# GpSimd makes the middle products of a bidirectional recurrence, and the decay's factor moves to ScalarE's exponential

## The reference

```python
tf = sigmoid(sum(time_emb, axis=-1))[:, None, None]
decay = exp(-exp(w))[None, :] * (0.5 + 0.5 * tf[:, :, 0])
ek = exp(minimum(k, 30.0));  ekv = ek * v
def step(carry, x):
    a, b = carry
    ekv_t, ek_t = x
    a = a * decay + ekv_t
    b = b * decay + ek_t
    return ((a, b), (a, b))
nf, df = scan(step, ..., (ekv_t, ek_t))                  # over the 256 time steps
nb, db = scan(step, ..., (ekv_t, ek_t), reverse=True)
euk = exp(minimum(u + k, 30.0))
num = nf + nb - ekv + euk * v
den = df + db - ek + euk
base = sigmoid(r) * (num / maximum(den, 1e-08))
out = base * (0.8 + 0.2 * tf)
```

## Time and profile before

| | |
|---|---|
| median of 3 runs | 372.89 us (369.75 to 375.7) |
| the profiled execution's own time | 368.91 us |
| its span on the core | 367.1 us |
| mean granted TensorE clock | 0.823 of full speed |

### The profile page before, as it was taken

How to read it: one execution, slowest core, us unless ns; L and a number is a source line. 1 busy time by engine, 2 the same in 40 slices (tenths; PEclk the granted TensorE clock), 3 DMA queues, 4 the chain that set the end, 5 groups by cost and what they waited for, 6 DMA issues and landing times.

```text
span 367.1 us, 6013 instructions
## 1 busy us (share of the span) xinstructions
PE 264.5 (72%) x2294; PEld 166.2 (45%) x2294; DVE 258.2 (70%) x494; ACT 207.4 (57%) x349; POOL 42.5 (12%) x70
## 2 busy tenths in 40 slices
PE   0053867899896888477885969769498499987645
PEld 0033434556554455244463546545266255565413
DVE  2989888779988999887699296774453535436671
ACT  3847598679859885245278257821675224452422
POOL 2102101021011113000310140103000000000000
PEclk9996586889999999887998598958789555698876
DMA  4905546345876530330036303603000000000000
GB/s 142 414 30 108 101 79 116 59 79 94 192 140 129 111 67 2 57 57 2 1 59 114 59 1 57 116 0 59 1 2 14 14 2 1 2 29 0 17 14 29
DMA packets 8524, 23.58 MB, mean 64 GB/s; under 512 B 1584, under 2 KB 2992, under 8 KB 8112
## 3 DMA queue, kind: packets, MB, share of 16 engines
q0 software_dynamic: 4320, 15.73, 22.7%
q1 hardware_dynamic: 4176, 7.48, 6.0%
HBM read 6.43 MB, written 1.05 MB: 20 GB/s over the span
## 4 chain that ended last, share of the span: by engine, by line
PE 44%; DVE 34%; ACT 11%; issue 9%; DMA 2%; POOL 1%; DVEq 0%; ACTq 0%; POOLq 0%
PE PS L1347 8%; DVE fwd L712 5%; PE PM L1264 5%; DVE bwd L720 4%; PE PO L1362 4%; PE PO L1461 3%; PE PS L1438 2%; PE PM L1090 2%; DVE kp L952 2%; PE PS L1326 2%; PE PO L1145 2%; PE PO L1378 2%; DVE fwd L1003 2%; PE PO L1160 2%; PE PO L1447 2%
## 5 line engine op out<-in xcount | busy, mean ns | idle before, releaser
L952 DVE TENSOR_REDUCE kp<-PS 128x2 f32<-128x256 f32 x64 | 32.3, 549 | 28.5 <-PE PS L1326 28.4
L639 ACT ACTIVATE E<-PS 128x384 f32<-128x384 f32 x64 | 27.9, 490 | 41.0 <-PE PS L1347 41.0
L523 ACT ACTIVATE E<-PS,negc,escale 128x1024 f32<-128x1024 f32 x32 | 38.3, 1201 | 4.7 <-PE PS L1130 4.5
L1090 PE MATMUL PM<-w,sg 128*128 128x256 f32 x32 | 11.3, 516 | 20.9 <-DVE sg L735 20.9
L1347 PE MATMUL PS<-w,TP 32*128 32x256 f32 (+1 forms) x128 | 20.8, 442 | 6.9 <-ACT E L639 6.9
L1145 PE MATMUL PO<-E,kp 128*32 128x256 f32 x256 | 20.3, 441 | 7.6 <-DVE ytok L810 4.1
L329 POOL DMA_DIRECT2D fwd<-bwd x15 | 13.4, 891 | 90.3 <-DVE bwd L720 53.4
L1130 PE MATMUL PS<-TP 32*128 32x256 f16 x256 | 20.3, 284 | 3.6 <-DVE TP L762 3.6
L1347 PEld LDWEIGHTS PS<-w,TP 32*128 32x128 f32 x128 | 15.7, 244 | 14.1 <-issue 9.2
L1264 PE MATMUL PM<-G,sg 128*128 128x512 f32 x32 | 20.1, 786 | 2.0 <-DVE sg L735 2.0
L323 POOL DMA_DIRECT2D fwd<-mid x15 | 13.4, 896 | 69.0 <-DVE fwd L712 69.0
(11 more groups left out here) (188 smaller groups left out, 591.9 us busy)
## 6 DMA issues: line engine op xcount, KB each, us to landing
fwd<-mid POOLq DMA_DIRECT2D x15, 512.0 KB, 4.6
fwd<-bwd POOLq DMA_DIRECT2D x15, 512.0 KB, 4.7
kT<-in_kT SPq DMA_DIRECT2D x4, 256.0 KB, 6.4
xT<-in_xT SPq DMA_DIRECT2D x4, 256.0 KB, 5.5
G<-in_w SPq DMA_DIRECT2D x1, 1024.0 KB, 8.6
vt<-in_w SPq DMA_DIRECT2D x1, 1024.0 KB, 10.4
G<-in_attn SPq DMA_DIRECT2D x1, 1024.0 KB, 6.6
out<-ek SPq DMA_DIRECT2D x8, 128.0 KB, 1.7
```

What stands on the lines that cost most here:

```text
L523: nc.scalar.activation(E[:, p % 6], PS[:, 2 * (p % 2):2 * (p % 2) + 2, :], ACT.Exp, bias=negc[:], scale=escale[:]).then_inc(S["e0_done"], 1)
L639: nc.scalar.activation(E[:, p % 4, i, 0:384], PS[:, i, 0:384], ACT.Exp, scale=QSCALE).then_inc(S["e1_done"], 1)
L952: nc.vector.tensor_reduce(kp[:, b % 2, u * H + 2 * j:u * H + 2 * j + 2, D], PS[:, at0:at0 + 2, lo:hi], AX, ALU.max, negate=True).then_inc( ...
L1090: ins = nc.tensor.matmul(PM[:, 0, u * C:(u + 1) * C], sg[:, seg(b, k * T + u * P, P)], w0[:, 0, k, :], start=(k == 0), stop=(k == HALF - 1))
```

## The change

The product `kT * mid` goes from DVE's `inputs(n)` to POOL's `add_mid(n)` for n = 2 to 15; for n = 0 and 1 it stays on DVE. The factor `fb` is taken out of all products, of `ekv` too, so that they are plain two-input multiplications. It comes back in the reciprocal: ACT's exponential gets the bias ln(fb), and the guard of the gate becomes fb times 1e8, read from a tile by partition. POOL makes `fbmax` and ACT makes `lnfb` once at the start.

```diff
             def add_mid(n):
-                r, o = n % RING, n % 2
+                r, o, b = n % RING, n % 2, n % B
+                if n >= 2:
+                    pool.wait_ge(S["m_done"], n + 1)
+                    nc.gpsimd.tensor_tensor(mid[:, o, 1], kT[:, seg(b)], mid[:, o, 0],
+                                            ALU.mult).then_inc(S["mv_done"], 1)
                 pool.wait_ge(S["mv_done"], n + 1)
                 pool.wait_ge(S["scan_done"], 4 * n + 2)
                 nc.gpsimd.dma_start(fwd[:, r], mid[:, o], accum_op=ALU.add).then_inc(S[f"mid_added{o}"], 16)
...
             nc.gpsimd.tensor_scalar(fb[:], cth[:], 0.05, 0.45, ALU.mult, ALU.add).then_inc(S["decay_ready"], 1)
+            pool.wait_ge(S["decay_ready"], 1)
+            nc.gpsimd.tensor_scalar(fbmax[:], fb[:], 1e8, None, ALU.mult).then_inc(S["fbmax_done"], 1)
             link(nc.gpsimd.tensor_scalar(dtf[:], cth[:], 0.25, 0.75, ALU.mult, ALU.add))
...
-                nc.scalar.activation(fwd[:, r, 0], fwd[:, r, 0], ACT.Exp, scale=-1.0).then_inc(S["rec_done"], 1)
+                nc.scalar.activation(fwd[:, r, 0], fwd[:, r, 0], ACT.Exp, bias=lnfb[:, b:b + 1],
+                                     scale=-1.0).then_inc(S["rec_done"], 1)
...
                     act.wait_ge(S["ln_bias"], 1)
+                    nc.scalar.activation(lnfb[:], fb[:], ACT.Ln).then_inc(S["lnfb_done"], 1)
+                    act.wait_ge(S["lnfb_done"], 1)
                     wkv(0)
...
-                nc.vector.scalar_tensor_tensor(G[l][:, seg(b)], fwd[:, r, 0], 1e8, fwd[:, r, 1], ALU.min,
+                    dve.wait_ge(S["fbmax_done"], 1)
+                nc.vector.scalar_tensor_tensor(G[l][:, seg(b)], fwd[:, r, 0], fbmax[:, b:b + 1], fwd[:, r, 1], ALU.min,
                                                ALU.mult).then_inc(S["gate_ready"], 1)
...
                     dve.wait_ge(S["ek_raw"], b + 1)
-                    dve.wait_ge(S["decay_ready"], 1)
                     link(nc.vector.tensor_scalar(ek[:, seg(b)], ek[:, seg(b)], EXP30, None, ALU.min))
-                    nc.vector.scalar_tensor_tensor(ekv[:, seg(b)], kT[:, seg(b)], fb[:, b:b + 1], ek[:, seg(b)],
-                                                   ALU.mult, ALU.mult).then_inc(S["ekv_done"], 1)
+                    nc.vector.tensor_tensor(ekv[:, seg(b)], kT[:, seg(b)], ek[:, seg(b)],
+                                            ALU.mult).then_inc(S["ekv_done"], 1)
                 dve.wait_ge(S["prep_done"], 3 * n + 2)
                 nc.vector.tensor_scalar(mid[:, n % 2, 0], mid[:, n % 2, 0], EXP30, None,
                                         ALU.min).then_inc(S["m_done"], 1)
-                dve.wait_ge(S["m_done"], n + 1)
-                nc.vector.scalar_tensor_tensor(mid[:, n % 2, 1], kT[:, seg(b)], fb[:, b:b + 1], mid[:, n % 2, 0],
-                                               ALU.mult, ALU.mult).then_inc(S["mv_done"], 1)
+                if n < 2:
+                    dve.wait_ge(S["m_done"], n + 1)
+                    nc.vector.tensor_tensor(mid[:, n % 2, 1], kT[:, seg(b)], mid[:, n % 2, 0],
+                                            ALU.mult).then_inc(S["mv_done"], 1)
```

More of the change, by code:

```diff
@@ L48 @@
     "cond_sum", "cond_tanh", "decay_exp", "ek_raw", "ekv_done", "decay_ready", "decay_edge", "prep_done",
-    "pool_chain", "dve_chain", "pads_set", "kp_clear",
+    "pool_chain", "dve_chain", "fbmax_done", "lnfb_done", "pads_set", "kp_clear",
     "m_done", "mv_done", "scan_done", "den_early", "num_early", "mid_added0", "mid_added1", "back_added0",
@@ L100, in build @@
         dtf = sb("dtf", [P, B])
+        fbmax = sb("fbmax", [P, B])
+        lnfb = sb("lnfb", [P, B])
         ew = sb("ew", [P, LAYERS, HALF])
```

## The result

| | before | after |
|---|---|---|
| time, median of 20 runs each (us) | 368.96 (366.06 to 375.83) | 372.65 (370.18 to 376.24) |
| ratio to before, 95% interval | | 1.0114 (1.0086 to 1.0142) |
| span of the profiled execution (us) | 367.1 | 370.9 |
| mean granted clock of TensorE | 0.823 | 0.813 |
| DVE busy (us) | 258.2 | 259.8 |

Some executions of any kernel fall in a slower state at a lower granted clock (5 of the 20 before, 1 of the 20 after); ratios leave them out, and so the plain medians differ by less, 3.7 us. The change costs 1.1%, 4.2 us. That is under the 2% up to which I had called it no change, but the interval starts at 0.9%, well clear of none. The predicted 372.6 us agrees with the 372.65 only because it stood on a median of three runs, 372.89, that was high: 20 runs of before have 368.96. What has to be compared is the difference, -0.3 us forecast and +4.2 measured.

What follows compares the result with a forecast made beforehand. The prediction took a chain of 44% PE and 34% DVE as the bound. Its terms, -4.7 + 0.35 - 0.07 + 0.3 + 3.8 = -0.3 us, on a median of 372.89 gave 372.6 us, range 367 to 378.

Steps and rivals of the forecast that it cites:

- What POOL's product costs DVE: POOL products of 1.1 us hold DVE's two-input SBUF work; +3.8 us in all, 6.2 at the upper bound.
- Rival (a): DVE held by POOL's products cancels the gain from moving them: 372.6 us, no change; chance 0.50.
- Where the products meet DVE: Costly meetings at n = 2, 6, 7, 9, 10, 11, mostly with scans and gates; n = 12 at 0.
- The price of one: One meeting of a POOL product with DVE's two-input work costs about 0.9 us, bounds 0 and 1.3.
- The relief: Products leaving DVE's part of the chain save 0.78 us each, six of them: -4.7 us.
- the six: Products of n = 2, 6, 7, 10, 11 and 12, the only ones counted on the chain, 0.78 us each.
- the other eight: Products of n = 3, 4, 5, 8, 9, 13, 14 and 15, whose leaving DVE was counted at nothing.
- Gate and fold: Gate limit read from a tile, +0.35 us; plain two-input products, -0.07; the exponential's bias costs nothing.
- The start: `fbmax` between `fb` and `dtf` on POOL delays the first scan 0.27 us; +0.3 with the first gate's 0.07.
- POOL's queue: The product delays add_mid(8) by 1.1 us and add_back(8) by at most that; 1.6 us of slack covers it.
- Rival (c): Slower: the product delays the DMA issued just ahead, add_back lands 1.1 to 1.45 us later; 376.5 us, chance 0.25.
- DVE busy: DVE's busy time in the profile after would fall to about 250 to 255 us, as blocked instructions count as busy.

Runs made afterwards that it cites:

- none_all: Kernel with all products on DVE, but those of n = 2 to 15 left out on every engine; ratio to the kernel before 0.993.
- fold_dve: Changed kernel with all 16 products back on DVE, the rest of the change kept; ratio to the kernel before 1.002, 369.50 us.
- fold_twin: fold_dve with POOL making each product of n = 2 to 15 once more into an unread tile; ratio to the kernel before 1.0449, 383.72 us.
- fold_fill: fold_dve with POOL filling an unread tile for n = 2 to 15, reading nothing from SBUF; ratio to the kernel before 1.0049.
- fold_copy: fold_dve with POOL multiplying one SBUF input by 1.0 into an unread tile for n = 2 to 15; ratio to the kernel before 1.0129.
- fold_start: fold_dve with the old start: `fbmax` made behind the decays, DVE's first clamp waiting for `fb`; ratio to the kernel before 1.001.
- timed_late: Changed kernel, old start, 1 MB load held back, 11 products on POOL timed to miss DVE's two-input SBUF reads, rest on DVE; ratio to before 1.0031, 367.18 us.
- after_spacer: Changed kernel with a one-element fill, waited for, ahead of each product on POOL; ratio to the kernel before 1.0036, 369.65 us.

## Why the prediction was wrong

The forecast of no change failed at the step **"What POOL's product costs DVE"**, the term of +3.8 us. That term took its meetings for the places where the leaving product lay in the chain, and its price from an add with no DMA issue ahead of it. Against none_all it measures 6.8 us, give or take 1.7, so even the lower end is above 3.8. The sum of the terms as measured: relief -3.3, fold with start and gate +0.7, blocks +6.8, together +4.2. (They add up by construction: none_all and fold_dve stand between before and after.)

- **The mechanism was right.** fold_twin, fold_fill and fold_copy show that POOL's reads hold DVE's two-input work, and instructions on the accumulators go free, as the earlier trace rows had it. Rival (a) named the mechanism that decides; its balance was wrong.
- **Where the products meet DVE.** I priced six meetings that cost something, for the values of n whose product lay in the chain and for n = 9. There were 11. For n = 4, 8, 13 and 15 I had written nothing, since the product's *leaving* gains nothing there. A block costs where it falls, and it falls on other instructions (scan, gate) than the one that left. n = 12 was to take the place of a collision that was there, at 0; a block of 0.77 came for the 0.35 that line 702 had lost to the adds. The five meetings that I had at nothing make 5.6 of the 11.2 us.
- **The price of one.** 0.9 us with a bound of 1.3, from 0.48 for an add of 0.72 in the earlier trace rows, was near the mean (11.2 over 11 is 1.02) and wrong at the top: 1.71, 1.35 and 1.75 right behind the issue of add_back. There the add of the earlier trace rows was no guide, for no DMA was issued ahead of it. At the six priced places 3.8 were predicted and 5.6 measured.
- **From durations to time** there is no fixed rate. In fold_twin 12.9 us of blocks cost 15.8 us, in the changed kernel 11.2 cost 6.8. Up to the clearing of `kp` the changed kernel is 8.8 us behind none_all, with 6.5 us of blocks by then. TensorE is granted less there as well (0.74 against 0.81 from 45 to 70 us, 0.94 against 1.00 from 100 to 120). What of the two is cause and what follows stays open.
- **The relief.** -4.7 predicted, -3.3 measured, give or take 2: not contradicted. That the six make up all of it isn't shown either: they gave 1.8 and the other eight 1.0, with the same error.
- **Gate and fold.** +0.35 and -0.07 with the start's 0.3 make 0.6; measured 0.7. The gate takes 0.74 to 0.75 instead of 0.68, as the row of another instruction with such an operand had it. That the bias costs nothing was wrong in the instruction: ACT's exponential takes 0.72 in all 16 places with a bias by partition and took 0.63 without, but it isn't seen in the time of fold_start, 1.001.
- **The start.** +0.27 predicted, 0.97 measured, 0.19 of it from the loads. "That DVE no longer waits for `fb` gains nothing" was too mild: the wait kept two engines apart, and without it `fb`, `fbmax` and `dtf` were stretched. I had applied the rule of the blocks to DVE alone, though the earlier trace rows shows POOL's adds stretched as well.
- **POOL's queue.** Add_mid(8) went out 1.9 us behind its place of none_all, counted from add_back(7) (2.46 against 0.54 us between the starts), for the 1.1 predicted. Add_back(8) went out 1.20 us after gate(7), before 1.29: the slack covered it, as said. Rival (c) forecast slower, by a later landing of add_back; that wasn't seen. The kernel is slower by another way, the blocks.
- **DVE busy.** 250 to 255 predicted, 259.8 measured: the same mis-sizing.

No version that makes all the products was faster than the kernel before. The best of the changed ones, timed_late and after_spacer, lie 0.3 to 0.4% above it with intervals that touch no difference.

## What to carry to other kernels

Before an elementwise instruction goes from VectorE to GpSimd, list for each of its copies what VectorE runs in the 1.3 us behind its new start, all along the program and not only where the old one was on the critical path; each two-input SBUF instruction there can cost the whole of the moved one (here up to 1.75 us for 1.26 behind a DMA issue), and here the blocks cost twice what the move freed. Leave the product out altogether first: if that gives 0.9%, another placement can't be expected to give more. A wait that looks useless may be what keeps the two engines out of each other's way.

## What was not expected of the hardware

- A GpSimd product queued right behind its DMA issue can hold a VectorE instruction that is listed ahead of it, by 0.23 us at 93.07 in the changed kernel and by 0.42 at 93.52 in fold_twin; these lost 1.71 and 1.88 us to a product of 1.26. With a one-element fill and a wait between them no scan lost more than 1.08.
- GpSimd's multiplication of 128x512 fp32 by a constant, one input, takes 1.49 us at least, its product of two such tiles 1.26.
- GpSimd's fills of 1.26 to 1.60 us leave VectorE's two-input scans as they are (1282 and 1214 ns).
- The hold works both ways, and on small instructions too: VectorE's 0.28 us `vr` took 2.16, GpSimd's 0.19 us `fb` took 0.71.
- ScalarE's exponential over 128x512 takes 0.72 us with a bias read by partition, 0.63 without.
